# Edge stage of a graph kernel: the e and w products in the step of their own transposes, the y products two steps behind

## The chip, the cores and the metric

The kernel runs on one core of one Trainium2 chip. The metric is the time of the whole program on the device in microseconds, as the median of three runs. Every time below is in microseconds unless it is marked ns.

## The reference, cut to what matters

One graph convolution with a residual and a layer norm, over 50,000 nodes (160 numbers each: 64 scalars and 32 vectors of three) and 50,000 edges, sorted by destination, all in float32:

```python
h = jax.nn.silu(edge_scalars @ (Wfc1 / jnp.sqrt(jnp.float32(FC_IN))))
w = h @ (Wfc2 / jnp.sqrt(jnp.float32(FC_H)))
f0 = x0 @ Wl1_0 * a * inv8
f1 = jnp.einsum('num,uv->nvm', x1, Wl1_1) * a[..., None] * inv32
e0 = f0[edge_src]
e1 = f1[edge_src]
mid0 = w0 * e0 * sh0
mid1 = w3 * jnp.einsum('eum,em->eu', e1, sh1) / jnp.sqrt(3.0)
mid2 = w1[:, :, None] * e0[:, :, None] * sh1[:, None, :]
mid3 = w2[:, :, None] * e1 * sh0[:, :, None]
# means of mid0..mid3 over the edges of each destination node: scal, vec
alpha = scal @ Wa * a * inv96
out_s = scal @ Wl2_s * a * inv96
out_v = jnp.einsum('num,uv->nvm', vec, Wl2_v) * a[..., None] * inv96
# result: layernorm(x + sc + alpha * concat(out_s, out_v)), sc a linear map of x
```

## The kernel before, in words

The work has two stages, one after the other in each engine's program, and each engine's instructions are written out by hand; semaphores join the engines. There is no scheduler: what an engine does next is the next instruction of its own program.

**Edge stage.** The edges are taken in 98 quads of 512 edges (NS = 98; a quad is two pairs, k = 0 and 1, of two tiles, t = 0 and 1, of 128 edges). For a quad q:

- GpSimd (POOL) issues four indirect DMAs, L586, which gather the rows of the source nodes into `gat`, a ring of four quads. Gather q waits for the transposes of quad q - 4.
- VectorE (DVE) prepares it (`prepare`, L944, L953, L959): a scaled copy `sha` of the edge attributes and a sum of products that it writes back into `gat`. It runs two quads ahead of the transposes.
- TensorE (PE) takes the first layer (`first_layer`, L669), and transposes both pairs (`turn`, L675 and L677) into PSUM. ScalarE (ACT) copies both out (`take_turned`): `h_sb` at L822 with silu, `t_sb` at L824, which releases `t_out`. Both buffers hold two quads.
- TensorE multiplies `t_sb` by the node weights into `e_ps` (`weigh`, L690 and L695), and `h_sb` by the second layer's weights into `w_ps` (L708). ScalarE copies e to `e_sb` (L847), and VectorE multiplies it by w into `mid` (`multiply`, L969).
- TensorE multiplies `mid` by the output weights into `y_ps` (`combine`, L726 and L728, once for each pair), ScalarE copies a part to `z` (`take_second`, L832), and VectorE makes the message of it (`finish`, L987 and L993; `label`, L977). SyncE (SP) stores the messages to `rows` in HBM (L413).

`edge_steps` runs `step(d)` on each engine for d from 0 to NS + 2. In step d the kernel before transposes quad d, weighs quad d - 1 at the step's end, multiplies quad d - 2 on VectorE, and combines and finishes quad d - 3. `between` puts single tasks between VectorE's steps: `prepare_order` (L1013 to L1017) after step 0, `take_heads` after step 1, and later tables of where each node's edges begin; on TensorE `spread_heads` (L747, L753) follows step 1. After VectorE's step 46 SyncE stores a table of single numbers, `starts_dram` (L451).

PSUM is shared: `e_ps` and `y_ps` of pair 0 lie in the same two banks, so that `combine` of pair 0 waits for the copies of e, and `weigh` waits for `finish` of pair 0.

**Node stage.** For each of 98 groups of 512 nodes, windows of message rows are loaded, summed by a product with a one-hot matrix (L787), added to a linear map of x, and normalised. Its first L787 waits for the last message. The change doesn't touch this stage.

Of the kernel before, what the change touches and what calls it, by code (L numbers as in the profile page):

```python
# [94 lines left out]
def gnn_kernel(nc, turned, spread, x_g, src_t, dst_t, dst_rows, sh_t, ea_t, weights, out):  # L95
# [4 lines left out]
    NS = T // QUAD  # L100
# [17 lines left out]
    with ExitStack() as ctx:  # L118
# [3 lines left out]
        def sem(name):  # L122
            return ctx.enter_context(nc.semaphore(name))
# [164 lines left out]
        e_ready = sem("e_ready")  # L288
        e_out = [sem(f"e_out{t}") for t in range(2)]
        w_ready = sem("w_ready")  # L290
        mid_ready = [sem(f"mid_ready{t}") for t in range(2)]
# [51 lines left out]

        def edge_steps(step, between={}):

            for d in range(NS + 3):
                step(d)
                if d in between:
                    between[d]()

        def alive(d, behind):

            return 0 <= d - behind < NS
# [302 lines left out]
        def _(pe):  # L656
# [57 lines left out]
            def combine(q, k):  # L714
                p, y = 2 * q + k, y_ps[k]
                if p == 1:
                    pe.wait_ge(heads_out, 2)
                for t in range(2):
                    if p == 0:
                        pe.wait_ge(wy_ready, 8)  # L720
                    pe.wait_ge(mid_ready[t], q + 1)
                    if k == 0:
                        pe.wait_ge(e_out[t], min(q + 2, NS))
                    if q >= 1:
                        pe.wait_ge(msg_ready[t], p - 1)
                    nc.tensor.matmul(y[:, t, 0:W_Y1 - W_YA], mid[:, q % 2, t, 0, k, :],  # L726
                                     wy[:, 0:W_Y1 - W_YA], start=True, stop=True)
                    nc.tensor.matmul(y[:, t, W_Y1 - W_YA:YW], mid[:, q % 2, t, 1, k, :],  # L728
                                     wy[:, W_Y1 - W_YA:W_SA - W_YA],
                                     start=True, stop=True).then_inc(y_ready[t], 1)  # L730

            def step(d):
                if alive(d, 0):
                    first_layer(d)
                for k in range(2):
                    if alive(d, 0):
                        turn(d, k)
                    if alive(d, 3):
                        combine(d - 3, k)
                if alive(d, 1):  # L740
                    weigh(d - 1)

            def spread_heads():

# [66 lines left out]
        def _(act):  # L811
# [14 lines left out]
            def take_second(q, k):  # L826
                p = 2 * q + k
                for t in range(2):
                    act.wait_ge(y_ready[t], p + 1)
                    if p >= 2:  # L830
                        act.wait_ge(msg_ready[t], p - 1)
                    nc.scalar.activation(z[:, k, t, 0:1 + MUL0], y_ps[k][:, t, Y_C:YW],  # L832
                                         ACT.Copy).then_inc(zc_ready[t], 1)

            def step(d):
                for k in range(2):
                    if alive(d, 0):
                        take_turned(d, k)
                    if alive(d, 3):
                        take_second(d - 3, k)  # L840
                if alive(d, 1):
                    q = d - 1
                    act.wait_ge(e_ready, q + 1)
                    for t in range(2):
                        if q >= 1:
                            act.wait_ge(mid_ready[t], q)
                        nc.scalar.activation(e_sb[:, t, :], e_ps[:, t], ACT.Copy  # L847
                                             ).then_inc(e_out[t], 1)

            edge_steps(step)  # L850

            def take_std(g):
# [22 lines left out]
            def step(i, b):  # L875
# [38 lines left out]
                elif old == NG - LAST_GROUPS:  # L914
# [4 lines left out]
                    normalise(old + 3, GROUP // 2)  # L919

            node_steps(act, step)


        @block.vector
        def _(dve):
# [37 lines left out]
            def multiply(q, t):  # L963

                dve.wait_ge(w_ready, q + 1)
                dve.wait_ge(e_out[t], q + 1)
                if q >= 2:
                    dve.wait_ge(y_ready[t], 2 * (q - 2) + 2)
                nc.vector.tensor_tensor(  # L969
                    mid[:, q % 2, t].rearrange("p c k e -> p (c k e)"), w_ps[:, t], e_sb[:, t],  # L970
                    ALU.mult).then_inc(mid_ready[t], 1)

            def label(q):
                half = slice(q % 2 * QUAD, (q % 2 + 1) * QUAD)
                if q >= 2:
                    dve.wait_ge(messages_out[q % 2], 16 * (q // 2))
                nc.vector.tensor_copy(msg[:, half, LABEL], dsts[:, QUAD * q:QUAD * (q + 1)]  # L977
                                      ).then_inc(label_ready, 1)
# [17 lines left out]
                        op0=ALU.mult, op1=ALU.add).then_inc(msg_ready[t], 1)  # L996

            def step(d):
                if alive(d, 2):
                    multiply(d - 2, 0)  # L1000
                if alive(d, 3):
                    label(d - 3)
                    finish(d - 3, 0)
                if alive(d, 2):
                    multiply(d - 2, 1)
                if alive(d, 3):
                    finish(d - 3, 1)
                if alive(d, -AHEAD):
                    prepare(d + AHEAD)

# [453 lines left out]
```

## Time and profile before

| | us |
|---|---|
| three runs | 939.92, 939.04, 938.84 (median 939.04) |
| the profiled execution's own time | 942.17 |
| its span, first to last instruction | 940.4 |
| mean granted TensorE clock, of full speed | 0.993 |
| busy: PE, PEld, DVE, POOL, ACT | 903.4, 799.0, 810.2, 712.5, 631.8 |

The span is what the profile shows; 1.8 us of the execution lie outside it. The profiled execution is 3.1 us longer than the median, so a difference that is worked out within the profile is carried over to the median as a difference. PE is TensorE's matmuls, PEld its weight loads. A float32 product is carried out as two passes, so that one instruction of the program stands in the trace as two matmuls and two weight loads. Over the whole page the edge stage takes about the first 557 us and the node stage the rest.

### The profile page before, as it was taken

Reading aid. Unit: us, or ns where it says so; the run is one execution under the profiler, and the core shown is the slowest. Engines: PE = TensorE matmul, PEld = TensorE weight load, DVE = VectorE, ACT = ScalarE, POOL = GpSimd, SP = SyncE. Lnnn points to the kernel's source line nnn. Section 1 sums busy time; section 2 is a strip of 40 time slices with the busy share of each in tenths; the row PEclk is TensorE's granted clock in tenths of the full one; section 3 lists DMA queues with packets and bytes.
Section 4 is the critical chain, followed back from the end, with each engine's and each line's share of the span. In section 5 each row is a group of like instructions: output and inputs, shape, how many; then the busy total and the mean of one; then the engine's idle time right before and its main releaser. Section 6 shows DMA issues by size and latency. Waiting matters only on the chain.

```text
span 940.4 us, 27168 instructions
## 1 busy us (share of the span) xinstructions
PE 903.4 (96%) x7944; PEld 799.0 (85%) x7944; DVE 810.2 (86%) x2793; ACT 631.8 (67%) x1961; POOL 712.5 (76%) x804
## 2 busy tenths in 40 slices
PE   2999999999999999999999989999999999999995
PEld 2788888888888888888888879998988889988994
DVE  3798899999989999888888977888888888888887
ACT  1555555555555555555555537898988888888887
POOL 6777777777777777767767317998888889888894
PEclk9999999999999999999999999999999999999998
DMA  6465554454465555456544217999999999999993
GB/s 176 118 177 153 160 141 129 131 139 130 134 120 163 157 166 139 130 157 178 143 132 127 82 75 215 313 297 308 302 292 298 294 290 304 302 311 301 306 293 142
DMA packets 87518, 186.34 MB, mean 198 GB/s; under 512 B 17646, under 2 KB 48138, under 8 KB 87371
## 3 DMA queue, kind: packets, MB, share of 16 engines
q1 hardware_dynamic: 48411, 87.64, 28.9%
q10 hardware_dynamic: 20016, 61.15, 19.6%
q0 software_dynamic: 18944, 35.81, 17.2%
q8 instruction: 66, 1.08, 0.5%
q14 instruction: 81, 0.66, 0.2%
HBM read 119.58 MB, written 64.95 MB: 196 GB/s over the span
## 4 chain that ended last, share of the span: by engine, by line
PE 64%; POOL 20%; issue 12%; DVE 2%; DMA 1%; POOLq 0%; ACT 0%; DVEq 0%; ACTq 0%
PE ps L728 12%; POOL res L639 9%; PE ps L690 9%; PE ps L708 9%; PE ps L726 8%; PE ps L695 6%; POOL xa L627 6%; PE ps L677 5%; PE ps L787 4%; PE ps L675 4%; POOL xa L623 3%; PE ps L797 2%; PE ps L669 2%; DMA gat<-spread,srcs 1%; PE ps L773 1%
## 5 line engine op out<-in xcount | busy, mean ns | idle before, releaser
L586 POOL DMA_INDIRECT gat<-turned,srcs x196 | 189.0, 964 | 74.5 <-issue 67.3
L586 POOL DMA_INDIRECT gat<-spread,srcs x196 | 189.1, 965 | 61.8 <-issue 56.0
L847 ACT ACTIVATE e_sb<-ps 128x512 f32<-128x512 f32 x196 | 106.4, 595 | 131.0 <-PE ps L695 131.0
L787 PE MATMUL ps<-win,hot 60*128 60x162 f32 x2352 | 190.5, 308 | 0.7 <-DVE hot L1310 0.7
L728 PE MATMUL ps<-wy,mid 128*128 128x161 f32 x784 | 182.3, 314 | 0.0
L787 PEld LDWEIGHTS ps<-win,hot 60*128 60x128 f32 x2352 | 166.4, 187 | 17.1 <-issue 16.5
L993 DVE SCALAR_TENSOR_TENSOR msg<-ps,sha,z 128x161 f32<-128x161 f32 x392 | 151.0, 385 | 13.9
L639 POOL TENSOR_TENSOR res<-agg,pre 128x640 f32<-128x640 f32 x98 | 151.9, 1550 | 11.4 <-ACT agg L892 11.4
L726 PE MATMUL ps<-wy,mid 128*128 128x97 f32 x784 | 141.4, 262 | 0.2 <-DVE mid L969 0.2
L969 DVE TENSOR_TENSOR mid<-ps,e_sb 128x512 f32<-128x512 f32 x196 | 133.1, 679 | 2.1 <-PE ps L708 2.1
L870 ACT ACTIVATE fin<-res,shift,rstd 128x160 f32<-128x160 f32 x292 | 132.0, 537 | 1.4 <-DVE shift L1259 1.3
L892 ACT ACTIVATE agg<-ps,coef 128x160 f32<-128x160 f32 x392 | 122.4, 407 | 8.4 <-DVE coef L1350 8.3
L726 PEld LDWEIGHTS ps<-wy,mid 128*128 128x128 f32 x784 | 123.2, 190 | 1.3 <-issue 0.7
L832 ACT ACTIVATE z<-ps 128x65 f32<-128x65 f32 x392 | 89.7, 229 | 46.0 <-PE ps L728 46.0
L728 PEld LDWEIGHTS ps<-wy,mid 128*128 128x128 f32 x784 | 119.0, 192 | 0.0
L797 PE MATMUL ps<-wy,xt 128*128 128x128 f32 x784 | 113.5, 288 | 0.2 <-DVE pre L1337 0.2
L987 DVE TENSOR_TENSOR z<-ps,sha 128x96 f32<-128x96 f32 x392 | 97.8, 250 | 15.7 <-ACT z L832 15.0
L797 PEld LDWEIGHTS ps<-wy,xt 128*128 128x128 f32 x784 | 94.8, 191 | 17.5 <-issue 17.5
L690 PE MATMUL ps<-t_sb,wt 128*128 128x256 f32 x392 | 103.0, 385 | 3.1 <-issue 3.1
L822 ACT ACTIVATE h_sb<-ps 128x128 f32<-128x128 f32 x196 | 54.3, 277 | 73.5 <-PE ps L677 62.4
L627 POOL TENSOR_TENSOR xa<-xin 128x512 f32<-128x512 f32 x98 | 102.5, 1046 | 0.0
L708 PE MATMUL ps<-h_sb,wt 64*128 64x256 f32 x784 | 101.1, 376 | 0.6 <-DVE mid L969 0.6
(105 smaller groups left out, 1611.9 us busy)
## 6 DMA issues: line engine op xcount, KB each, us to landing
win<-rows SPq DMA_DIRECT2D x392, 114.6 KB, 3.6
rows<-msg SPq DMA_DIRECT2D x98, 326.0 KB
out<-fin ACTq DMA_DIRECT2D x47, 640.0 KB, 5.3
xin<-x_g ACTq DMA_DIRECT2D x92, 322.0 KB, 4.5
gat<-turned,srcs POOLq DMA_INDIRECT x196
gat<-spread,srcs POOLq DMA_INDIRECT x196
eas<-ea_t SPq DMA_DIRECT2D x7, 384.0 KB, 5.3
xin<-x_g SPq DMA_DIRECT2D x6, 322.0 KB, 4.0
```

What stands on the lines that cost most here:

```text
L586: pool.indirect_dma_start(out=gat[:, slot, first:first + of.shape[1]], out_offset=None, in_=of, in_offset=bass.IndirectOffsetOnAxis(ap=src ...
L627: nc.gpsimd.tensor_tensor(xa[:, b0, 0:GROUP, :], xin[:, n, :, 1:1 + P], xin[:, n, :, 0:1].broadcast_to([P, GROUP, P]), ALU.mult).then_inc( ...
L639: nc.gpsimd.tensor_tensor(res[:, slot], agg[:, b3], pre[:, b3], ALU.add).then_inc(res_ready, 1)
L690: nc.tensor.matmul(e_ps[:, t, 2 * P:4 * P], wt[:, W_E1:W_E1 + P], t_sb[:, b, 1 + t].rearrange("p k e -> p (k e)"), start=True, stop=True)
L708: last = nc.tensor.matmul(w_ps[:, t, 2 * c * P:2 * (c + 1) * P], wt[half, w:w + P], h_sb[half, b].rearrange("p k e -> p (k e)"), start=Tru ...
L726: nc.tensor.matmul(y[:, t, 0:W_Y1 - W_YA], mid[:, q % 2, t, 0, k, :], wy[:, 0:W_Y1 - W_YA], start=True, stop=True)
L728: nc.tensor.matmul(y[:, t, W_Y1 - W_YA:YW], mid[:, q % 2, t, 1, k, :], wy[:, W_Y1 - W_YA:W_SA - W_YA], start=True, stop=True).then_inc(y_r ...
L787: last = nc.tensor.matmul(agg_ps[b1][:, 2 * h + k, 0:SW], hot[side(h), b1, k, c, :], win[side(h), (b - 1) % RING, k, c, 0:SW], start=c == ...
L797: nc.tensor.matmul(sca_ps[:, k, :], xt[:, b1, k, :], wy[:, W_SA - W_YA:W_SB - W_YA], start=True, stop=True)
L870: last = nc.scalar.activation(fin[:, past, k, :], res[:, past, k, :], ACT.Identity, bias=shift[:, past, k:k + 1], scale=rstd[:, past, k:k ...
L969: nc.vector.tensor_tensor(mid[:, q % 2, t].rearrange("p c k e -> p (c k e)"), w_ps[:, t], e_sb[:, t], ALU.mult).then_inc(mid_ready[t], 1)
L993: nc.vector.scalar_tensor_tensor(out=msg[:, q % 2 * QUAD + n, 0:1 + D], in0=y[:, t, Y_A:Y_C], scalar=sha[:, ring, n, 0:1], in1=z[:, k, t, ...
```

## The change

Only the offsets between quads and steps change. `weigh(d)` now stands in step d, behind `turn(d, 0)` and `turn(d, 1)`, where it was `weigh(d - 1)`; VectorE multiplies quad d - 1; `combine`, `take_second`, `label` and `finish` take quad d - 2, where they took d - 3; and the loop runs to NS + 1. Of the transposes, the first layer, the preparation and the gathers nothing is moved. No instruction is added or removed and no size is changed.

```diff
         def edge_steps(step, between={}):
 
-            for d in range(NS + 3):
+            for d in range(NS + 2):
                 step(d)
...
                 for k in range(2):
                     if alive(d, 0):
                         turn(d, k)
-                    if alive(d, 3):
-                        combine(d - 3, k)
-                if alive(d, 1):
-                    weigh(d - 1)
+                    if alive(d, 2):
+                        combine(d - 2, k)
+                if alive(d, 0):
+                    weigh(d)
...
                     if alive(d, 0):
                         take_turned(d, k)
-                    if alive(d, 3):
-                        take_second(d - 3, k)
-                if alive(d, 1):
-                    q = d - 1
-                    act.wait_ge(e_ready, q + 1)
+                    if alive(d, 2):
+                        take_second(d - 2, k)
+                if alive(d, 0):
+                    act.wait_ge(e_ready, d + 1)
                     for t in range(2):
-                        if q >= 1:
-                            act.wait_ge(mid_ready[t], q)
+                        if d >= 1:
+                            act.wait_ge(mid_ready[t], d)
...
             def step(d):
+                if alive(d, 1):
+                    multiply(d - 1, 0)
                 if alive(d, 2):
-                    multiply(d - 2, 0)
-                if alive(d, 3):
-                    label(d - 3)
-                    finish(d - 3, 0)
+                    label(d - 2)
+                    finish(d - 2, 0)
+                if alive(d, 1):
+                    multiply(d - 1, 1)
                 if alive(d, 2):
-                    multiply(d - 2, 1)
-                if alive(d, 3):
-                    finish(d - 3, 1)
+                    finish(d - 2, 1)
                 if alive(d, -AHEAD):
                     prepare(d + AHEAD)
```

TensorE at the start of the edge stage, before: the first two steps and what follows them (the names in brackets are the semaphores that an instruction waits for).

```order
L675 MATMUL ps<-ident,gat 128x128 [waits q_ready]
L677 MATMUL ps<-ident,gat 128x128 x2
L669 MATMUL ps<-eas,wt 128x128 [waits t_out,h_out]
L669 MATMUL ps<-eas,wt 128x128
L675 MATMUL ps<-ident,gat 128x128 [waits q_ready]
L677 MATMUL ps<-ident,gat 128x128 x2
L675 MATMUL ps<-ident,gat 128x128 [waits q_ready]
L677 MATMUL ps<-ident,gat 128x128 x2
L690 MATMUL ps<-t_sb,wt 128x256 [waits t_out]
L690 MATMUL ps<-t_sb,wt 128x256
L695 MATMUL ps<-t_sb,wt 128x256 x2
L708 MATMUL ps<-h_sb,wt 128x256 [waits h_out]
```

The same place now, from the second pair of quad 0 on:

```order
L675 MATMUL ps<-ident,gat 128x128 [waits q_ready]
L677 MATMUL ps<-ident,gat 128x128 x2
L690 MATMUL ps<-t_sb,wt 128x256 [waits t_out]
L690 MATMUL ps<-t_sb,wt 128x256
L695 MATMUL ps<-t_sb,wt 128x256 x2
L708 MATMUL ps<-h_sb,wt 128x256 [waits h_out]
L708 MATMUL ps<-h_sb,wt 128x256 x3
L669 MATMUL ps<-eas,wt 128x128 [waits t_out,h_out]
L669 MATMUL ps<-eas,wt 128x128
L675 MATMUL ps<-ident,gat 128x128 [waits q_ready]
```

The eight products of quad 0 (L690, L695, L708) stand ahead of quad 1's first layer and transposes, where they stood behind them.

VectorE at the same place, before, from the last task of `prepare_order` to the first message:

```order
L1017 TENSOR_REDUCE wrong<-res 128x1 [waits greater_ready]
L944 TENSOR_TENSOR sha<-shs,gat 128x16 [waits gathered14,gathered15,gathered13,gathered12]
L953 TENSOR_TENSOR qprod<-gat,sha 128x384 [waits sha_ready,q_ready]
L959 TENSOR_REDUCE gat<-qprod 128x4x32 [waits qprod_ready]
L1023 COPY heads_all<-ps 128x392 [waits wrong_summed,heads_spread]
L1024 COPY wrong_sum<-ps 1x1
L969 TENSOR_TENSOR mid<-ps,e_sb 128x512 [waits e_out0,w_ready]
L969 TENSOR_TENSOR mid<-ps,e_sb 128x512 [waits e_out1,w_ready]
```

And now (the lines of this part of the file are one lower than before):

```order
L1016 TENSOR_REDUCE wrong<-res 128x1 [waits greater_ready]
L968 TENSOR_TENSOR mid<-ps,e_sb 128x512 [waits e_out0,w_ready]
L968 TENSOR_TENSOR mid<-ps,e_sb 128x512 [waits e_out1,w_ready]
L943 TENSOR_TENSOR sha<-shs,gat 128x16 [waits gathered14,gathered15,gathered13,gathered12]
L952 TENSOR_TENSOR qprod<-gat,sha 128x384 [waits sha_ready,q_ready]
L958 TENSOR_REDUCE gat<-qprod 128x4x32 [waits qprod_ready]
L1022 COPY heads_all<-ps 128x392 [waits wrong_summed,heads_spread]
```

Both multiplications of quad 0 move ahead of the preparation of quad 3 and of `take_heads`. In the middle of the stage the forms of the instructions of a step and their order are the same before and after on TensorE, ScalarE and VectorE; only the quad that they belong to differs, relative to the transposes.

## Rows read from the trace of the kernel before

**Rows 1.** Busy time by stretch: PE, PEld, DVE, ACT, POOL, granted clock, DMA, GB/s.

```profile
400.00:500.00 100.00, 100.00 (x781) 88.18 (x779) 89.25 (x261) 57.60 (x188) 70.20 (x75) 1.00 0.54 150
```

**Rows 2.** Timeline of one undisturbed step: start, length, engine, line, [idle before].

```profile
436.90 0.39 PE L669 MATMUL ps<-eas,wt 64*128 64x128 f32 x4
...
439.30 0.48 ACT L824 ACTIVATE t_sb<-ps 128x384 f32<-128x384 f32 x1
...
439.62 0.47 PE L728 MATMUL ps<-wy,mid 128*128 128x161 f32 x2
...
439.79 0.76 PEld L690 LDWEIGHTS ps<-t_sb,wt 128*128 128x128 f32 x4
...
439.92 1.03 PE L690 MATMUL ps<-t_sb,wt 128*128 128x256 f32 x4
```

**Rows 3.** Timeline, first groups of the node stage: TensorE released by ScalarE.

```profile
557.64 0.27 ACT L884 ACTIVATE xt<-ps 128x128 f32<-128x128 f32 x1
...
557.97 0.53 PEld L773 LDWEIGHTS ps<-ident,xa 128*128 128x128 f32 x5 [1.09 <-ACT xt L884]
```

**Rows 4.** Timeline, one step where VectorE is late; last, the page's row of L690.

```profile
353.63 1.09 PE L690 MATMUL ps<-t_sb,wt 128*128 128x256 f32 x4
...
354.02 0.30 PEld L690 LDWEIGHTS ps<-t_sb,wt 128*128 128x128 f32 x2 [0.20 <-DVE msg L993]
...
L690 PE MATMUL ps<-t_sb,wt 128*128 128x256 f32 x392 | 103.0, 385 | 3.1 <-issue 3.1
```

**Rows 5.** Timeline of the first step: another release of TensorE by ScalarE.

```profile
14.76 0.48 ACT L824 ACTIVATE t_sb<-ps 128x384 f32<-128x384 f32 x1
...
15.36 0.53 PEld L669 LDWEIGHTS ps<-eas,wt 64*128 64x128 f32 x4 [1.21 <-ACT h_sb L822]
```

**Rows 6.** Timeline of the start of the edge stage.

```profile
22.80 0.56 DVE L1017 TENSOR_REDUCE wrong<-res 128x1 f32<-128x392 f32 x1
...
24.43 0.93 PE L747 MATMUL ps<-heads,ones 1*128 1x196 f32 x4
...
25.41 0.49 PE L669 MATMUL ps<-eas,wt 64*128 64x128 f32 x4
...
27.40 1.27 DVE L969 TENSOR_TENSOR mid<-ps,e_sb 128x512 f32<-128x512 f32 x2
...
28.81 1.14 PE L708 MATMUL ps<-h_sb,wt 64*128 64x256 f32 x8 [0.60 <-DVE mid L969]
...
29.75 0.42 PE L669 MATMUL ps<-eas,wt 64*128 64x128 f32 x4
...
38.88 1.03 PE L690 MATMUL ps<-t_sb,wt 128*128 128x256 f32 x4
```

**Rows 7.** Timeline of PEld, first loads of the weighings of quads 95 to 97.

```profile
538.28 0.76 PEld L690 LDWEIGHTS ps<-t_sb,wt 128*128 128x128 f32 x4
...
543.66 0.76 PEld L690 LDWEIGHTS ps<-t_sb,wt 128*128 128x128 f32 x4
...
548.20 0.76 PEld L690 LDWEIGHTS ps<-t_sb,wt 128*128 128x128 f32 x4
```

**Rows 8.** Timeline: weighings of quads 12 and 16, VectorE's waits for gathers between.

```profile
87.14 0.54 PEld L690 LDWEIGHTS ps<-t_sb,wt 128*128 128x128 f32 x3
...
90.07 0.17 DVE L944 TENSOR_TENSOR sha<-shs,gat 128x16 f32<-128x16 f32 x1 [1.06 <-DMA gat<-spread,srcs]
...
101.83 0.17 DVE L944 TENSOR_TENSOR sha<-shs,gat 128x16 f32<-128x16 f32 x1 [1.39 <-DMA gat<-spread,srcs]
...
110.12 0.54 PEld L690 LDWEIGHTS ps<-t_sb,wt 128*128 128x128 f32 x3
```

**Rows 9.** Timeline: SyncE's store of the table, and VectorE's wait for gather 50.

```profile
269.85 0.40 SPq L451 DMA_DIRECT2D starts_dram<-starts  x1
...
280.58 0.18 DVE L944 TENSOR_TENSOR sha<-shs,gat 128x16 f32<-128x16 f32 x1 [1.75 <-DMA gat<-spread,srcs]
```

**Rows 10.** Busy time by stretch, columns as in rows 1, first groups of the node stage.

```profile
559.00:563.00 4.00, 3.58 (x26) 3.44 (x27) 1.46 (x5) 0.53 (x2) 1.28 (x2) 0.57 0.00 1
```

## The prediction, written before the changed kernel ran

> **What bounds the kernel now.** I read first the busy time by stretch. In the middle of the edge stage TensorE is busy for all of the 100 us from 400 to 500, at a granted clock of 1.00, while VectorE has 89 and GpSimd 70 [rows 1]. Busy alone proves little for an engine whose matmul ends are modelled, so I read next the timeline of one undisturbed step [rows 2]: between the last L728 and the first L690 there is no gap, and L669, the first work of the step, is followed by the next quad's L690 3.02 us later (436.90 to 439.92). The weighings of quads 95 and 96 start 5.38 us apart [rows 7]; that is the period of the stage, and it is TensorE's own work. So the edge stage lasts as long as TensorE's instructions plus whatever TensorE waits for, and the reader has four places to look at: what makes TensorE wait in the middle of a step, what it waits for at the start, what stands in the last steps, and the steps in which another engine is late.
>
> The order of the instructions shows that in the middle of the stage only one relation changes. `multiply` still follows the weighing by one step and `combine` still follows `multiply` by one, on all engines; the copies of e, the z copies, the messages and their stores keep their distance to `weigh`. What gets closer is `turn` and `weigh`: the wait of the first L690 for `t_out`, which was a whole step old, is now for the t_sb that ScalarE has just written. The node stage is untouched and starts with the last message, so whatever the edge stage gains or loses goes to the end.
>
> **The wait that is now fresh, in each step.** Behind the second pair's transposes TensorE has `combine` of pair 1. Over that time ScalarE writes h_sb and t_sb, and t_sb ends at 439.30 + 0.48 = 439.78; the first load for L690 begins at 439.79, and its matmul at 439.92 [rows 2]. So the data is ready within 0.01 of the moment at which the load starts today, in every undisturbed step. What is added is the time from ScalarE's end to TensorE's load. The nearest row is a TensorE load that ScalarE did release, L773: ScalarE's L884 ended at 557.64 + 0.27 = 557.91, the load starts at 557.97 [rows 3]: 0.05 to 0.06. The load would start about 0.05 later than now, still 0.08 ahead of its matmul's turn. How much of that is covered is told by a step in which VectorE released the second L690 late [rows 4]: the load came at 354.02, the matmul that needs it had its turn 0.04 later (353.63 plus two spacings of 0.216, three of which and one duration of 0.38 make the 1.03 of the undisturbed group in rows 2), and the group took 1.09 in place of 1.03. A load only 0.04 ahead thus cost 0.06, so a load must be about 0.10 to 0.11 ahead to cost nothing. Ours will be 0.08 ahead: a loss of 0.02 to 0.03. I take 0.02. The bounds are nothing (if the weight load is fully hidden) and 0.06 (if nothing hides it).
>
> The Trainium skill, TensorE: Matmul & The Clock Gate, section LDWEIGHTS (loading the stationary operand), gives a load as its columns divided by 1.2 in ns, 107 ns for 128 columns; no row prints that time by itself (the trace's loads are 0.19 long). An estimate by it would be 0.107 - 0.08 = 0.03 us of loss a step, and a sum about 0.6 us less favourable than mine.
>
> The loss falls on the steps that are undisturbed, about 88 of 98; where TensorE waits longer for VectorE or a gather, the release is hidden in that wait. 88 x 0.02 = +1.8 us, with bounds 0 and 88 x 0.06 = 5.3.
>
> **The start.** Before, TensorE transposes quad 0, then waits for quad 1 with nothing to do, and everything that follows is behind the first L708 of quad 1, which waits at 28.81 for the multiplications of quad 0, which VectorE takes at 27.40, after `prepare_order`, the preparation of quad 3 and `take_heads` [rows 6]. Now the weighing of quad 0 runs in that idle time, and VectorE multiplies quad 0 directly behind L1017, which ends at 22.80 + 0.56 = 23.36. The two multiplications take 1.27, to 24.63; TensorE's L708 of quad 1 follows 0.14 later (28.81 against 27.40 + 1.27), at 24.77. The next group starts 0.94 behind it (29.75 - 28.81), at 25.71: that is `spread_heads`, which takes 0.98 (24.43 to 25.41). L669 of step 2 starts at 26.69. Step 2 now holds `combine` of quad 0, so it takes 3.02 to its L690: 29.71, and with the release above 29.73. One full step later, at 29.73 + 5.40 = 35.13, the weighing of quad 3 starts. In the profile before it starts at 38.88 [rows 6]. That is -3.75 us. VectorE can follow: `take_heads` ends where it does now, the multiplication of quad 1 starts at 27.40, that of quad 2 one step of 5.38 later at 32.78, and w of quad 2 is written by 29.73 + 2.36 (5.38 - 3.02) + 0.3 = 32.4. The gathers go on at GpSimd's own pace, since the ring is not full yet.
>
> **The end.** Before, the last weighing stood in a step without transposes and came 548.20 - 543.66 = 4.54 after the one before it, where a full step takes 5.38 [rows 7]. Now all weighings stand in full steps: +0.84. Behind the last weighing both programs have the same two combines, multiplications and messages. The step that is saved is therefore not 5.38 us: its instructions are still executed, elsewhere. It is the start's idle time that is filled.
>
> **Late gathers.** Quads 12 to 16 are weighed in 110.12 - 87.14 = 22.98, where four steps take 21.52: 1.46 lost. In between VectorE waits 1.06 and 1.39 for gathers [rows 8], which are late because GpSimd sets its constants there. GpSimd runs at its own pace at that point. Relative to the transposes of the same quad the start gives back less than a step: weighing 3 is in step 3 and not 4, and comes 3.75 earlier, so step d as a whole is 5.38 - 3.75 = 1.6 later, and some 1.9 by step 13 with the release. VectorE comes to each preparation 1.9 later against the same gathers, more than the 1.06 and 1.39: the waits go. -1.4, with bounds -1.46 and 0. The wait for gather 50, 1.75 long, comes from the table store at 269.85, which lands together with it at 280.6 [rows 9]; the store is tied to the same steps as the gather, so I leave it, though the messages of quad 44 now queue right behind it: 0, with bounds -1.1 and +1.5.
>
> **The sum.** -3.75 (start) + 0.84 (end) + 1.8 (release) - 1.4 (gathers) = -2.5, I round to -2.4. Against the profiled execution's own 942.17 that is 939.8. That execution is 3.1 above the median of 939.04; the difference carries over, and the median comes to 936.6.
>
> **Rivals.**
>
> A. TensorE's clock takes back half of the start. TensorE now works from 15.3 on, waits from about 23 to 24.77 for VectorE, and is thinly used before. In this trace the clock was granted at the full level (2.4 GHz) through the whole middle, but fell to the lower level (1.2 GHz) at the node stage's first groups, after a stretch in which TensorE was busy for about half of the time: 0.57 in the 4 us from 559 [rows 10]. If it is at or falls to 1.2 GHz over quad 1's w and step 2, up to 3.4 us of work are done at half speed, and the start gives 1.7 less: -0.7, 938.3. For it: the gap. Against it: TensorE was busy nearly without a pause from 15.3 to 23.
> The Trainium skill, same page, section What's actually happening, says that the clock depends on how busy TensorE has been recently. By that rule this rival is real; the trace agrees for the node stage.
>
> B. The gathers stay late. If the 1.9 us is less, because step 2 waits for something I missed, or the landings move with the messages stored earlier, 1.4 isn't gained: -1.0, 938.0.
>
> C. Nothing hides the release. At 0.05 to 0.06 in each step the loss is 4.4 to 5.3 in place of 1.8, and the sum +0.2 to +1.1: 939.2 to 940.1, 939.6 in the middle. Against it are rows 4.
>
> D. Slower: the release costs much more than a semaphore's 0.05. In the first step ScalarE's t_sb ended at 14.76 + 0.48 = 15.24 and the TensorE load that waited for it (and for h_sb) began at 15.36 [rows 5], 0.12 later. If L690 is released like that, because it has other semaphores beside t_out and the waits are served one after another, its load is 0.11 late, only 0.02 ahead of its turn, and costs 0.11 - 0.03 = 0.08 to 0.09: 88 x 0.09 = 7.9 in place of 1.8, +3.7 in all, 942.7. It decides from a loss of 0.07 a step on. For it: the row. Against it: there two separate waits had to be passed freshly, while here the other semaphores of L690 (msg_ready, e_out) come in before t_out.
>
> **How the numbers follow.** The measurement tells about 0.2% from no change, 1.9 us: faster is below 937.2, slower above 940.9. My forecast has 0.50 (936.6), A 0.13, B 0.18, C 0.08, D 0.11. The forecast's own spread is about 1.2 us to each side, so some of it is within 0.2%, and some of A and B is below it; these about cancel. Faster 0.50, same 0.39, slower 0.11. The range of 8 in 10 reaches from 935.2 (no loss from the release, gathers all gained) to 939.6 (A, B and the middle of C) and leaves D out.
>
> **What would show it.** In the changed kernel's trace: the first L690 at about 15.3; the load for L690 in the middle steps 0.05 behind the end of t_sb, now with a short idle before it, and the period 5.40 in place of 5.38; the weighing of quad 3 at about 35.1; VectorE's preparations of quads 15 and 17 without a wait for a gather; the weighing of quad 97 about 2.4 before 548.20, by an undisturbed 5.40 behind that of 96; the node stage as long as before. The prediction is wrong if the period grows by 0.05 or more, if the clock is low after 23 us, or if a wait appears at L977 (messages not yet stored) or at a gather in a new place.

## The result and the profile after

The changed kernel took 945.6 us (median of 4 runs, 944.1 to 946.89), the kernel before on the same chip 939.37 (4 runs, 938.84 to 939.92). The ratio is 1.0054, with a 95% interval of 1.0029 to 1.008: slower by 0.54%, where 936.6 was predicted. The profiled execution of the changed kernel took 944.87 (span 943.1), that of before 942.17 (span 940.4). Of the gap of 6.2 between the medians 2.7 are left between these two, because before's profiled execution was a long one, by its node stage: 383.1 against 380.6 in the profile after. There TensorE's granted clock stood at 0.50, its lower level (1.2 GHz), for 3.4 us from 559.0 on [rows 10], and after it was 1.00 over the same groups (562.5 to 566); by an estimate, half of 3.4, that is 1.7 of the 2.5. So the comparison below is made within the edge stage, up to the last message: 557.29 before, 562.49 after, +5.20.

The middle of the stage, the busy time by stretch after: PE, PEld, DVE, ACT, POOL, granted clock, DMA, GB/s. It is as in [rows 1].

```profile
400.00:500.00 100.00, 100.00 (x777) 88.06 (x778) 89.21 (x262) 56.90 (x185) 70.53 (x75) 1.00 0.53 148
```

The timeline of one undisturbed step after, against [rows 2], and the page's row of L690, against that of [rows 4] (start, length, engine, line, idle before; the page's row: busy, mean ns, idle before):

```profile
437.88 0.48 ACT L824 ACTIVATE t_sb<-ps 128x384 f32<-128x384 f32 x1
...
438.42 0.73 PEld L690 LDWEIGHTS ps<-t_sb,wt 128*128 128x128 f32 x4
438.51 1.05 PE L690 MATMUL ps<-t_sb,wt 128*128 128x256 f32 x4
```

```profile
L690 PE MATMUL ps<-t_sb,wt 128*128 128x256 f32 x392 | 105.7, 392 | 9.3 <-issue 7.5
```

The load now follows the end of t_sb (438.36) by 0.06, over the trace by 0.052, and is 0.09 ahead of its matmul, where it was 0.13 ahead. The group of four matmuls takes 1.05 for 1.03, and the weighings of the undisturbed steps are 5.398 apart for 5.378.

The timeline of the start after, against [rows 6]:

```profile
15.31 1.22 PE L690 MATMUL ps<-t_sb,wt 128*128 128x256 f32 x2 [0.75 <-ACT t_sb L824]
...
22.93 1.28 DVE L968 TENSOR_TENSOR mid<-ps,e_sb 128x512 f32<-128x512 f32 x2
...
24.35 1.13 PE L708 MATMUL ps<-h_sb,wt 64*128 64x256 f32 x8 [0.66 <-DVE mid L968]
...
29.52 1.05 PE L690 MATMUL ps<-t_sb,wt 128*128 128x256 f32 x4
...
34.91 1.05 PE L690 MATMUL ps<-t_sb,wt 128*128 128x256 f32 x4
```

The weighing of quad 3 is at 34.91 where it was at 38.88; between the loads, which have come closer to their matmuls, the distance is 3.92 (34.83 and 38.75). The granted clock, last but two in each row, stayed at its full level there:

```profile
14.80:23.00 8.20, 6.71 (x32) 4.73 (x32) 5.17 (x14) 2.76 (x8) 6.21 (x7) 1.00 0.47 148
23.00:27.00 4.00, 3.34 (x25) 2.25 (x25) 2.85 (x7) 1.09 (x2) 3.09 (x4) 1.00 0.30 76
27.00:36.00 9.00, 9.00 (x70) 7.98 (x70) 7.89 (x26) 5.09 (x18) 6.77 (x8) 1.00 0.42 111
```

The last weighings, loads on PEld, against [rows 7]: the last interval is a full step of 5.40 for 4.54.

```profile
548.03 0.73 PEld L690 LDWEIGHTS ps<-t_sb,wt 128*128 128x128 f32 x4
553.43 0.73 PEld L690 LDWEIGHTS ps<-t_sb,wt 128*128 128x128 f32 x4
```

VectorE's wait for a gather, against the two of [rows 8]; one of 1.33 is left.

```profile
97.39 0.17 DVE L943 TENSOR_TENSOR sha<-shs,gat 128x16 f32<-128x16 f32 x1 [1.33 <-DMA gat<-spread,srcs]
```

And the place that decides, in four views: SyncE's timeline (against [rows 9], where the table L451 left at 269.85), VectorE's, the loads of the weighings of quads 47 to 49, and the clock in the stretch at the end of the wait, with the first matmuls behind it.

```profile
264.78 0.44 SPq L446 DMA_DIRECT2D rows<-pads  x1
271.48 0.40 SPq L451 DMA_DIRECT2D starts_dram<-starts  x1
271.92 15.47 SPq L413 DMA_DIRECT2D rows<-msg  x3
```

```profile
283.92 0.17 DVE L976 COPY msg<-dsts 128x4 f32<-128x4 f32 x1 [6.89 <-DMA rows<-msg]
```

```profile
273.25 0.73 PEld L690 LDWEIGHTS ps<-t_sb,wt 128*128 128x128 f32 x4
284.76 1.35 PEld L690 LDWEIGHTS ps<-t_sb,wt 128*128 128x128 f32 x4 [6.10 <-issue]
292.25 0.73 PEld L690 LDWEIGHTS ps<-t_sb,wt 128*128 128x128 f32 x4
```

```profile
282.50:289.00 6.50, 4.21 (x14) 3.04 (x16) 4.21 (x13) 0.97 (x2) 0.37 (x1) 0.50 0.55 189
...
284.79 2.04 PE L690 MATMUL ps<-t_sb,wt 128*128 128x256 f32 x4 [5.89 <-issue]
```

SyncE issues the table and, 0.44 later, the messages of quad 44. These had been ready since 270.00, but SyncE's program waits for the table's values first, so their store leaves 1.92 late as well. VectorE's label of quad 46 writes into the same half of the message buffer, would have come at 277.03, and waits 6.89 for that store. TensorE, which waits for VectorE's messages before it may weigh, then has intervals of 11.50 and 7.49 where the step is 5.40. The first is the wait, 6.10 too long. The second, 2.09 too long, is the clock: TensorE stood idle from 278.9 to 284.8, and from 282.3 to 289.1 its granted clock was 0.50 in place of 1.00. It is busy without a pause from 284.79 on, and its first group takes 2.04 for 1.05. The table itself takes 10.5 to land:

```profile
starts_dram<-starts SPq DMA_DIRECT2D x1, 2.0 KB, 10.5
```

Compare SyncE's timeline before, directly behind the table of [rows 9]:

```profile
273.49 5.70 SPq L413 DMA_DIRECT2D rows<-msg  x2
```

There the messages of quad 44 left 3.64 behind the table, and the label of quad 46 came at 282.56, without a wait. Table and label are the same instructions in the same order; only their distance changed. The table is tied to VectorE's step 46, and the label of quad 46 moved from step 49 to step 48, as the message store of quad 44 moved from the end of step 47 to that of step 46. Before, the label came 2.6 after the table had landed (269.85 + 10.1 = 279.95). After, it came 4.95 before it (271.48 + 10.5 = 281.98), and the store behind the table needed 1.9 more: 6.9. Before, too, the store behind the table was slow. By the semaphore counts in the trace it landed at 282.54, 9.05 after its issue and 2.6 after the table, and the label came 0.02 later, itself put off by VectorE's wait of 1.75 for gather 50. So the kernel before had no room left at this place, and its missing wait doesn't show that.

The whole edge stage, before to after, from the intervals between weighings:

| part | predicted | measured |
|---|---|---|
| start, up to the weighing of quad 3 (loads) | -3.75 | -3.92 |
| release, 76 steps undisturbed in both | +1.8 | +1.56 (0.0206 each) |
| late gathers, steps 12 to 15 (22.97 to 22.31) | -1.4 | -0.67 |
| the table, steps 45 to 48 (22.77 to 29.93) | 0 (-1.1 to +1.5) | +7.16 |
| end, last interval | +0.84 | +0.85 |
| the other steps | 0 | +0.23 |
| sum | -2.5 | +5.2 |

Of the 29.93 of steps 45 to 48 after, 8.34 are above four steps of 5.398: 6.10 of the wait, 2.09 of the clock, and 0.14 of the two steps ahead of it. Before, 1.26 were above four of 5.378; the release in the four steps, 0.08, makes up the +7.16.

### The profile page after: what moved, and what is told of

Its sections match the earlier page's. It is cut to its first block, busy times and chain, and to the rows that moved or that the text cites. A ratio compares the mean times of both kernels' runs of the same rounds, so it can differ in the third digit from the quotient of the medians.

```text
span 943.1 us, 27168 instructions
## 1 busy us (share of the span) xinstructions
PE 904.6 (96%) x7944; PEld 800.7 (85%) x7944; DVE 810.6 (86%) x2793; ACT 631.9 (67%) x1961; POOL 711.0 (75%) x804
## 4 chain that ended last, share of the span: by engine, by line
PE 67%; POOL 17%; issue 11%; DMA 2%; DVE 1%; POOLq 0%; ACT 0%; ACTq 0%; DVEq 0%
PE ps L728 12%; PE ps L690 9%; PE ps L708 9%; PE ps L726 8%; POOL res L639 8%; PE ps L695 6%; PE ps L787 6%; POOL xa L627 5%; PE ps L677 4%; PE ps L675 4%; PE ps L797 3%; POOL xa L623 3%; PE ps L669 2%; PE ps L773 2%; POOL fin L648 1%
## 5 line engine op out<-in xcount | busy, mean ns | idle before, releaser
L690 PE MATMUL ps<-t_sb,wt 128*128 128x256 f32 x392 | 105.7, 392 | 9.3 <-issue 7.5
L708 PE MATMUL ps<-h_sb,wt 64*128 64x256 f32 x784 | 102.3, 380 | 0.7 <-DVE mid L968 0.7
```

What stands on the lines that cost most here:

```text
L690: nc.tensor.matmul(e_ps[:, t, 2 * P:4 * P], wt[:, W_E1:W_E1 + P], t_sb[:, b, 1 + t].rearrange("p k e -> p (k e)"), start=True, stop=True)
L708: last = nc.tensor.matmul(w_ps[:, t, 2 * c * P:2 * (c + 1) * P], wt[half, w:w + P], h_sb[half, b].rearrange("p k e -> p (k e)"), start=Tru ...
```

## Experiments

All but the second and the eighth and tenth start from the changed kernel. Ratios are to the kernel before in the same job, with their 95% interval. "Last message" is its end in the profiled execution, 557.29 in before and 562.49 in after.

**e1: the table behind the messages of quad 44, not ahead of them.**

```diff
+            def store_starts():
+                sp.wait_ge(starts_ready, 1)
+                with nc.allow_non_contiguous_dma(...):
+                    sp.dma_start(starts_dram..., ...).then_inc(starts_out, 16)
             def store_messages(i):
...
                     ).then_inc(messages_out[half], 16)
+                    if i == STARTS // 2 and half == 0:
+                        store_starts()
...
-                    sp.wait_ge(starts_ready, 1)
-                    with nc.allow_non_contiguous_dma(...):
-                        sp.dma_start(starts_dram..., ...).then_inc(starts_out, 16)
```

> The changed kernel with one difference: SyncE issues the store of the table of starts (L451) behind the store of the messages of quad 44 and no longer ahead of it, so that the table again has about one step to itself before the next message store, as in the kernel before. Theory Q (queue order: the messages of quad 44 lie behind the table's 10 us in SyncE's queue, and VectorE's label of quad 46 waits 6.9 for them): the wait is gone, the edge stage is 7 us shorter than in the changed kernel, and the whole is 1.5 to 2 below the kernel before: 937 to 938. Rival S (the closer steps make the whole stage tighter, and the label's wait only shows it): 943 or more, with waits elsewhere.

Measured: 937.02 (12 runs), ratio 0.998 [0.9962, 0.9998]. Last message 554.15. SyncE's timeline:

```profile
269.50 0.35 SPq L419 DMA_DIRECT2D rows<-msg  x1
270.93 0.39 SPq L412 DMA_DIRECT2D starts_dram<-starts  x1
274.57 11.85 SPq L419 DMA_DIRECT2D rows<-msg  x3
```

The wait for the message store is gone. The same bytes go through the same queue at nearly the same time, with the messages of quad 44 ahead and those of quad 45 3.6 behind. What stays beside the table is one wait of 1.0 for a gather, where before has 1.75. Against after, 8.3 of the edge stage are back, 8.0 of them in steps 45 to 48 (21.95 for 29.93), and the clock stays at 1.00 through the whole edge stage.

**e2: the kernel before, with the table one step later relative to the messages.** This puts into before the distance that the change made: the table leaves after step 47 with the store of quad 44 right behind it.

```diff
-STARTS = 44
+STARTS = 45
```

> The kernel before with the table's tasks one step later (STARTS 45 for 44), so that the table is stored at the end of VectorE's step 47, directly ahead of the messages of quad 44, with a step of 5.4 until they are needed. Theory Q: the kernel before gets the same wait, some 6 to 7 us at the label of quad 46, and is 6 to 7 slower: 945 to 946. Rival S: within 0.5 us of before.

Measured: 946.86 (6 runs), ratio 1.0077 [1.0055, 1.0099]. SyncE's timeline, and VectorE's waits (total, times, longest):

```profile
275.04 0.40 SPq L451 DMA_DIRECT2D starts_dram<-starts  x1
275.48 3.50 SPq L413 DMA_DIRECT2D rows<-msg  x2
```

```profile
DVE msg L977 <- DMA rows<-msg: 6.8, 1, 6.8
```

The kernel before gets the same wait (6.8 for 6.9) and intervals of 11.49 and 7.19, with none of the change's other parts; the clock falls to 0.50 here too, for 6.8 us from 285.3 on. So the loss comes with the place of the table, and needs nothing else of the change. It was 0.9 more than the 945 to 946 expected.

**e3: the table from ScalarE's queue, at the same time.** Is it the order within SyncE's queue, or are the DMA engines busy with 512 small writes?

```diff
                     sp.wait_ge(starts_ready, 1)
-                    with nc.allow_non_contiguous_dma(...):
-                        sp.dma_start(starts_dram..., ...).then_inc(starts_out, 16)
...
-            edge_steps(step)
+            edge_steps(step, {46: store_starts})    # on ScalarE: act.wait_ge, act.dma_start
```

> The changed kernel with the table's store issued from ScalarE's queue at the end of its step 46; SyncE still waits for the table's values before it stores the messages of quad 44, so both are issued within 0.5 us of each other as in the changed kernel. Theory Q1 (the messages are late because they lie behind the table in the same queue): the label's wait goes to 0 or nearly so, 938 to 939.5. Rival Q2 (the table's 512 single numbers keep the DMA engines themselves busy, whatever queue they are in): a wait of 3 to 7 us at the label stays, 942 to 946.

Measured: 940.4 (12 runs), ratio 1.001 [0.9988, 1.0031]; last message 555.50. The two stores start together (SyncE's message store at 270.87), and VectorE's waits are:

```profile
270.88 0.43 ACTq L849 DMA_DIRECT2D starts_dram<-starts  x1
```

```profile
DVE msg L979 <- DMA rows<-msg: 1.3, 1, 1.3
DVE sha L946 <- DMA gat<-spread,srcs: 0.5, 1, 0.5
```

Out of the queue, the table costs the message store 1.3 and not 6.9. Most is the order of one queue; a smaller part, 1.3 for the store and 0.5 for a gather, stays. It is not settled whose that part is. SyncE still waits for the table's values, so that the store leaves 1.37 later than in e1 (269.50), and it still lands only 7.6 after its issue, where a store with nothing slow beside it lands in 2.5 (276.93 to 279.38 in e5, by the semaphore counts). The Trainium skill, DMA: Bandwidth & Descriptors, section Queues, rings and completion order, says that SyncE and ScalarE each have a ring of their own on each of the same 16 DMA engines, and that a ring's descriptors are taken in order; these two numbers agree with both halves. The span is 3.0 longer than e1's (936.9 against 933.9), of which 1.35 lie in the edge stage; in the node stage the clock was 0.50 from 557.8 to 561.2, and 1.00 there in e1. The median is above the 938 to 939.5 expected.

**e4: e1, and ScalarE writes t_sb ahead of h_sb.** It takes the new release off the path.

```diff
+                nc.scalar.activation(t_sb..., t_ps[:, k], ACT.Copy).then_inc(t_out, 1)
                 nc.scalar.activation(h_sb..., ACT.Silu, ...).then_inc(h_out, 1)
-                nc.scalar.activation(t_sb..., t_ps[:, k], ACT.Copy).then_inc(t_out, 1)
```

> As the kernel with the table behind the messages of quad 44, and ScalarE writes t_sb before h_sb for each pair. The release of L690 by t_out costs 0.021 us a step in the changed kernel (period 5.398 for 5.377), 1.9 in all. Theory: t_sb ends 0.17 earlier, its release is fully hidden, the period is 5.377 again, and the kernel is 1.9 below the one without this edit: 935 to 936. Rival: h_out, now later, or the earlier read of PSUM delays TensorE elsewhere, and the period stays at 5.40 or grows.

Measured: 936.4 (9 runs), ratio 0.9964 [0.9947, 0.998]; last message 553.81. One step on its timeline:

```profile
440.20 0.49 ACT L826 ACTIVATE t_sb<-ps 128x384 f32<-128x384 f32 x1
440.86 0.76 PEld L694 LDWEIGHTS ps<-t_sb,wt 128*128 128x128 f32 x4
441.00 1.03 PE L694 MATMUL ps<-t_sb,wt 128*128 128x256 f32 x4
```

t_sb ends 0.17 ahead of the load, the load is 0.14 ahead of its matmul, the group takes 1.03 again and the period is 5.378. So the 0.02 a step was the release. Its worth in time, 0.6 against e1 where 1.9 was expected, is less than these medians can tell; in the edge stages a gather that was 0.5 late at steps 14 and 15 and a longer wait for the gather behind the table took most of the 1.6 back.

**e5: a short table, directly ahead of the messages.** The table is turned by a product with the identity on TensorE and copied by VectorE after step 47, so that it is stored as 4 rows of 512 bytes, not as 512 single numbers; it stands ahead of quad 45's messages.

```diff
+            def store_starts():
+                sp.wait_ge(starts_taken, 1)
+                sp.dma_start(starts_dram.rearrange("(c p) -> c p", p=P), starts_t[:]
+                             ).then_inc(starts_out, 16)
...
                 for half in range(2):
+                    if i == STARTS // 2 and half == 1:
+                        store_starts()
...
-                    sp.wait_ge(starts_ready, 1)
-                    with nc.allow_non_contiguous_dma(...):
-                        sp.dma_start(starts_dram..., ...).then_inc(starts_out, 16)
...
+            def turn_starts():    # TensorE, after step 47
+                ...
+                nc.tensor.matmul(starts_ps, starts[:], ident[:], start=True, stop=True
+                                 ).then_inc(starts_turned, 1)
...
+                if d == STARTS + 3:    # VectorE, after step 47
+                    dve.wait_ge(starts_turned, 1)
+                    nc.vector.tensor_copy(starts_t[:], starts_ps).then_inc(starts_taken, 1)
```

> The changed kernel with the table of starts turned by one product on TensorE (128 x 4 to 4 x 128, copied out by VectorE after its step 47) and stored as four rows of 512 bytes in place of 512 single numbers, directly ahead of the messages of quad 45 in SyncE's queue. Theory Q: what delays the messages is the length of the table's store, 10 us of single numbers, and not its place: with the store short (2 to 4 us) the label of quad 47 waits 0 to 0.5 though the table is directly ahead of its messages, and the whole is as fast as with the table behind the messages or a little faster: 936 to 937.5. Rival P (any store that SyncE holds back until the table's values are there makes the messages late, by the holding back of up to 1.6): a wait of 2 or more stays at the label, 939 or more.

Measured: 935.76 (12 runs), ratio 0.9959 [0.9942, 0.9976]; last message 554.50. SyncE's timeline:

```profile
276.61 0.27 SPq L415 DMA_DIRECT2D starts_dram<-starts_t  x1
276.93 9.75 SPq L424 DMA_DIRECT2D rows<-msg  x3
```

The table is 0.32 ahead of the message store, nearer than the 0.44 in after, and the label that needs this store comes 5.87 behind it (282.80) without a wait on it. So it isn't a store ahead in the queue that costs, but one of 512 single numbers. Nor is it that SyncE holds the store back until the table is ready: these messages were ready at 275.03 and left 1.90 late, as in after. No gather is late at this place either; the product and the copy cost one step of 5.91. The hardware queue of SyncE has 47891 packets for 48411. The Trainium skill, same page, section Rules for kernel authors, says that a last dimension that isn't contiguous becomes one descriptor for each element, and to rearrange it; the packets agree.

**e6: the short table behind quad 45's messages, and t_sb first.**

> The short table, stored behind the messages of quad 45, and t_sb written before h_sb. If the wait for a gather beside the table's store (1.75 in the kernel before, 1.0 and 1.8 with the table behind the messages) comes from the table's single numbers, it is gone as well: no step longer than 5.6 around quad 48, period 5.378, 934.5 to 935.5, which is below both kernels by 0.4% or more. If it comes from the message stores alone, the wait stays and the time is that of t_sb first alone, 936.4.

Measured: 936.17 (12 runs), ratio 0.9972 [0.9949, 0.9995]; last message 553.34, period 5.377. This is the earliest last message of all, 1.16 before e5's, and yet the time is that of e5 and e4 within their spread, above the 934.5 to 935.5 expected. The 1.5 of the release doesn't show in the medians. No gather is late beside the short table, as in e5, so the late one in the other kernels goes with the single numbers; the step of 5.89 there is the product and the copy.

**e7: the changed kernel again, beside e5 and e6.**

> The changed kernel itself once more, beside the others on the same chip: both theories expect 944 to 946, the wait of some 6.9 at the label of quad 46, and a period of 5.398.

Measured: 944.38 (10 runs), ratio 1.0048 [1.0028, 1.0067], with a wait of 6.2 at the label and intervals of 10.80 and 8.25. The result comes again. Its profiled execution, the longest of the ten, also lost 5.2 at the start: the weighing of quad 3 is at 39.99 for 34.83 (loads), and the second interval 13.21 for 7.50. Gathers landed later (behind the first, VectorE waits 4.9 for them where it waited 3.7), TensorE stood for 2.47 ahead of its next loads of L708 where it stood for 1.0, and its clock went to 0.50 for 10.2 us from 24.8 on:

```profile
27.00:36.00 9.00, 9.00 (x40) 7.78 (x41) 4.72 (x15) 2.22 (x8) 6.87 (x8) 0.55 0.33 78
```

By an estimate, half of the 10.2, the clock is 5.1 of it. That is rival A of the prediction in the same kernel, in one execution out of two profiled.

**e8 and e9: which part of e5's gain is the change?** e8 is the kernel before with e5's table, e9 is e5 beside it.

> The kernel before with e5's short table (turned by one TensorE product after step 47, copied by VectorE, stored as 4 rows of 512 bytes directly ahead of the second half of the pair of quads 44 and 45). What is e5's gain over before: the change of the offsets, or the table? Theory T1 (mostly the change): in before the table costs only the wait for gather 50, about 1.1 us in the weighings 44 to 50, of which the product and the copy give back some 0.5 (in e5 a step of 5.91 at 47); this kernel is 0.3 to 1.1 faster than before, about 938.5 to 939.2, and the changed kernel with the same table is about 2 to 3 us faster still (start -3.9, end +0.85, release +1.8, gathers 0 to -1.4). Theory T2 (mostly the table): this kernel comes within 1 us of e5, about 936 to 936.5, and the change of the offsets is worth nothing that can be measured.

> The same kernel as e5, beside e8 on the same chip, so that their ratio is the change of the offsets alone. T1: 936 +- 0.7, 2 to 3 us under e8, weighing of quad 3 at about 35.0 against 38.8, period 5.398 against 5.378, last interval 5.40 against 4.54. T2: within 1 us of e8.

Measured: 1078.64 and 1078.47 (12 runs each), but the kernel before took 1078.61 in this job too (ratios 0.9997 [0.9965, 1.0029] and 0.9994 [0.9963, 1.0025]), for 939.4 to 941.3 in the others. In both traces the step is 6.6 and TensorE is not busy all the time; e8's row, its two largest waits of those 40 us, and a copy of ScalarE behind the transposes of its pair:

```profile
340.00:380.00 40.00, 35.33 (x259) 28.41 (x258) 29.99 (x88) 16.60 (x60) 22.82 (x25) 1.00 0.39 111
```

```profile
ACT h_sb L838 <- PE ps L684: 12.1, 6, 2.1
POOL gat L593 <- PE ps L684: 11.5, 6, 2.0
```

```profile
339.29 0.38 PE L684 MATMUL ps<-ident,gat 128*128 128x128 f32 x2
...
341.28 0.28 ACT L838 ACTIVATE h_sb<-ps 128x128 f32<-128x128 f32 x1 [2.03 <-PE ps L684]
```

ScalarE starts 1.61 after the end of these transposes, where it is 0.03 in before (437.77 to 437.80), at a full granted clock; from quad 94 on, when GpSimd has issued its last gathers, the steps are 5.38 and 5.40 again. Whatever made it so, TensorE's own work was not the bound there, and with intervals of 0.3% to each side, some 3 us, the runs say nothing on the question. Its cause wasn't followed up.

**e10 and e11: the same pair again.**

> e8 once more. In the job of e8 and e9 every kernel, the kernel before included, took about 1078.6, with a step of 6.61 in place of 5.38 wherever GpSimd still gathered, so it said nothing on the question. Where the kernel before takes its 939 to 940 again, T1 (e5's gain is mostly the change of the offsets) gives 938.5 to 939.2 here, T2 (mostly the table) 936 to 936.5. If the step of 6.6 comes again, it is a property of this kernel's place or chip, and the question stays open.

> e9 (the same kernel as e5) once more, beside e10. T1: 936 +- 0.7, 2 to 3 us under e10. T2: within 1 us of e10.

Measured, with the kernel before at 941.32 (18 runs): e10 940.03 (12 runs, 937.89 to 942.57), ratio 0.9986 [0.9968, 1.0003]; e11 936.03 (7 runs, 934.73 to 939.17), ratio 0.9937 [0.9915, 0.9959]. T2 is refuted and T1 stands in its main point: the short table gives before at most a little, and the change of the offsets is worth 4.0 between the medians once the table is short, more than T1's 2 to 3. The profiles show 1.94 of it in the edge stage: last message at 556.46 and 554.52, weighing of quad 3 at 39.03 and 35.16 (-3.87), 77 steps undisturbed in both +1.47, last interval +0.86 (4.54 to 5.40; loads of quads 96 and 97, of e10 and of e11):

```profile
542.82 0.76 PEld L697 LDWEIGHTS ps<-t_sb,wt 128*128 128x128 f32 x4
547.36 0.76 PEld L697 LDWEIGHTS ps<-t_sb,wt 128*128 128x128 f32 x4
```

```profile
540.05 0.73 PEld L697 LDWEIGHTS ps<-t_sb,wt 128*128 128x128 f32 x4
545.45 0.73 PEld L697 LDWEIGHTS ps<-t_sb,wt 128*128 128x128 f32 x4
```

Another 1.4 of the two spans' difference lies in the node stages (381.55 and 380.11), which the change doesn't touch, and I can name no interval for it. The node stages of single executions of one kernel or another lie between 379.6 and 383.1, so a pair of profiles doesn't settle what of the medians' 4.0 is the change.

## Why the prediction was wrong, step by step

- **What bounds the stage.** Right: TensorE in every undisturbed step, and which relation becomes fresh.
- **The release.** Right: 0.05 from ScalarE's end to the load, 0.0206 lost a step (0.02 predicted), and e4 takes it away again. An estimate by the load time of the Trainium skill (TensorE: Matmul & The Clock Gate, section LDWEIGHTS (loading the stationary operand)) was 0.03, and the trace has less. It fell on some 80 steps for 88, +1.6 for +1.8.
- **The start.** Right in mechanism and size: -3.92 for -3.75, in this execution. VectorE's first multiplications came 0.4 earlier than worked out (22.93), because `prepare_order` ran earlier too.
- **The end.** Right: +0.85 for +0.84.
- **Late gathers.** Half: -0.67 for -1.4. One of two waits went. This term was read from one execution: late gathers fall on other steps in other profiles (a late one at step 6 in e1, 0.4 to 1.1 of excess at step 14 in e4, e5 and e6, none in e3 or e7), also in before's order (steps 2 and 8 in e2, step 14 in e10). It should have stood as 0 to -1.4 with no value in the middle.
- **The table.** This step failed: "the store is tied to the same steps as the gather, so I leave it, though the messages of quad 44 now queue right behind it: 0, with bounds -1.1 and +1.5". It measured +7.16, and turned -2 into +5: the wait of 6.9 at the label of quad 46, for the store behind the table, made one interval 6.1 too long, and half the clock behind that wait the next one 2.1, less 1.26 that the place had cost before. The relation was seen and not priced. The price was in reach of the trace of before: the table takes 10.1 to land (269.85 to 279.95), and the label of quad 46 stood 2.6 behind that. The messages of quad 44 would be issued directly behind the table (270.29), and the label of step 48 stood 5.1 behind that, at 275.35. Had I assumed that the store lands no sooner than the table ahead of it, the wait was 10.1 - 0.4 - 5.1 = 4.6 or more; with the 2.6 by which that store landed behind the table before, 7.2. e1 (taken out), e2 (put into before), e3 (other queue) and e5 (short store in the same place) show the cause of the wait from four sides. That the clock falls behind it is seen in all three profiles with the wait (after, e2, e7) and in the edge stage of none of e1, e3, e4, e5, e6, e10 and e11; the 2.1 is read from the interval. The prediction did name what would refute it, "a wait appears at L977 (messages not yet stored)", and that is what appeared, now at L976.
- **Rivals.** A, the clock: in this execution it stayed at 1.00 over the start, no loss; in e7's it fell there for 10.2 us, so that its absence was partly luck. The fall that counts in the result, 2.1, is at the table, where no rival had it. B: half true, as above. C and D, an unhidden or long release: refuted by 5.398. D's 942.7 is on the right side, but its mechanism isn't there. The slower case that came true was none of the four. It belonged among them, with the one place where the change moves a step past work that stays where it is.

Without the table the terms add up to -1.9 where -2.5 was predicted (rounded there to -2.4), and e1, e5 and e11 are faster than before by 2.6, 3.7 and 5.3 between medians.

The versions to keep are the changed kernel with a short table (e5, 935.76, the same kernel as e9 and e11) or with t_sb first as well (e6, 936.17); e4, 936.4, needs no new instruction. The runs don't tell these apart. All are faster than both kernels.

## What to carry to other kernels

When a software pipeline is shifted against something that doesn't shift with it (here a table, stored once, tied to one engine's step number), list for every queue which pairs of transfers get closer, and price each by the landing time of the first, and of what stands behind it, against the due time of whoever waits for the second. A wait that is missing in the trace before doesn't show that there is room: look how long before the use the transfer landed. A store of single numbers in the queue of a large store belongs behind it, in another queue, or turned into rows. And a term that rests on a late transfer in one profiled execution is a range, not a value.

## What the runs showed of the hardware that I had not expected

- A store of 2 KB as 512 single numbers took 10.1 and 10.5 us to land, and a message store issued 0.44 behind it in the same queue landed 12.0 after its own issue (271.92 to 283.92). With the table on ScalarE's queue the message store had landed by 7.6 (270.87, label at 278.52), with 4 rows of 512 bytes ahead of it within 5.87. A message store 3.6 behind the table caused no wait at the label (e1, before), though before it took 9.05 to land.
- TensorE stood idle for 5.9 us (278.9 to 284.8) on one wait, and in it the granted clock fell to 0.50; the step behind the wait took 7.49 for 5.40. A wait of 6.9 so cost 8.2.
- A weight load 0.09 ahead of its matmul cost 0.02 (period 5.398), one 0.13 to 0.14 ahead nothing (5.378 in before and e4).
- One job ran all kernels 15% longer, with a step of 6.6 wherever GpSimd gathered. In it a saving of 2 to 4 us on TensorE's path couldn't be measured (0.9994 against 0.9997, each with an interval of 0.3% to each side). What it was is open.
